# Peak products of the 64-wide cross attention as pairs of 64-row operands into both banks, with one maximum over two banks

## What is computed

```
heads, dim_head = (16, 64)
x = layer_norm(x, ln_m_g, ln_m_b)              # context, 2 x 4096 x 256
lat = layer_norm(latents, ln_l_g, ln_l_b)      # 2 x 256 x 256
q = lat @ Wq
kv_input = jnp.concatenate([x, lat], axis=1)   # 4352 keys
k, v = jnp.split(kv_input @ Wkv, 2, axis=-1)
dots = jnp.einsum('bhid,bhjd->bhij', q, k) * dim_head ** (-0.5)
attn = jax.nn.softmax(dots, axis=-1)
out = jnp.einsum('bhij,bhjd->bhid', attn, v)
```

## Time and profile before

| what | value |
|---|---|
| median of 3 runs | 4079.12 us (4075.48 to 4081.56) |
| the profiled execution's own time | 4080.47 us |
| span of its instructions | 4078.7 us |
| TensorE (PE) busy | 3406.9 us, 84% |
| VectorE (DVE) busy | 2315.1 us, 57% |
| ScalarE (ACT) busy | 1529.1 us, 37% |
| GpSimd (POOL) busy | 810.1 us, 20% |
| peak products L1259 | 191.0 us busy, 576 weight loads |
| their maxima L1428 | 374.8 us busy, x576 |
| mean granted TensorE clock | 0.908 of full |

### The profile page before, as it was taken

One profiled execution on the slowest core, in us unless ns is written; L12 is line 12 of the kernel. 1 busy time (PEld: TensorE's weight loads), 2 busy tenths in 40 slices (PEclk: granted clock), 3 DMA queues, 4 the chain that ended last, 5 costly groups with the idle time before them and its releaser, 6 DMA issues. The chain is left out here.

```text
span 4078.7 us, 55851 instructions
## 1 busy us (share of the span) xinstructions
PE 3406.9 (84%) x21132; PEld 2130.0 (52%) x21188; DVE 2315.1 (57%) x3897; ACT 1529.1 (37%) x2241; POOL 810.1 (20%) x572
## 2 busy tenths in 40 slices
PE   7878895999999699999759587899857579995759
PEld 5546684656656466566525375444446434442225
DVE  1144413655655656656368413899654279984963
ACT  2223311334334243343246321467633137773311
POOL 0000000254255152453218202000000110000420
PEclk9888897999999799999879788999977789997879
DMA  2245463000000100000187513765200285540001
GB/s 94 85 142 181 166 238 140 16 6 6 6 1 1 55 6 9 4 4 1 30 272 260 218 68 105 164 122 106 50 21 26 103 205 114 120 81 21 0 22 59
DMA packets 223953, 339.07 MB, mean 83 GB/s; under 512 B 104272, under 2 KB 177680, under 8 KB 218064
## 3 DMA queue, kind: packets, MB, share of 16 engines
q1 hardware_dynamic: 223312, 334.56, 28.1%
q0 software_dynamic: 384, 1.05, 0.1%
HBM read 257.95 MB, written 77.63 MB: 82 GB/s over the span
## 5 line engine op out<-in xcount | busy, mean ns | idle before, releaser
L1428 DVE TENSOR_REDUCE L1x_pk<-L1x_psm 128x1 f32<-128x512 f32 (+1 forms) x576 | 374.8, 661 | 177.1 <-PE L1x_psm L1259 170.0
L1229 POOL TENSOR_TENSOR L1x_acc<-L1x_acc,L1x_pr 128x512 f32<-128x512 f32 x256 | 416.4, 1627 | 137.3 <-ACT L1x_pr L1404 118.9
L1404 ACT ACTIVATE L1x_pr<-L1x_pss 128x1024 f32<-128x1024 f32 x272 | 278.6, 1024 | 285.4 <-PE L1x_pss L1316 277.8
L1450 DVE TENSOR_TENSOR L1x_acc<-L1x_acc,L1x_pr 128x512 f32<-128x512 f32 x256 | 261.1, 1020 | 202.0 <-ACT L1x_pr L1404 197.6
L955 DVE TENSOR_REDUCE L2x_pk<-L2x_psm 128x1 f32<-128x512 f32 x512 | 328.1, 685 | 38.1 <-PE L2x_psm L792 34.3
L955 DVE TENSOR_REDUCE L3x_pk<-L3x_psm 128x1 f32<-128x512 f32 x512 | 328.1, 685 | 32.5 <-PE L3x_psm L792 28.7
L932 ACT ACTIVATE L2x_pr<-L2x_pss 128x1024 f32<-128x1024 f32 x256 | 248.2, 1021 | 105.6 <-PE L2x_pss L833 105.3
L932 ACT ACTIVATE L3x_pr<-L3x_pss 128x1024 f32<-128x1024 f32 x256 | 248.1, 1021 | 100.6 <-PE L3x_pss L833 100.3
L1316 PE MATMUL L1x_pss<-L1x_Q,L1x_K 64*128 64x256 f32 x2176 | 279.3, 376 | 0.0
L1282 PE MATMUL L1x_pss<-L1x_w,L1x_cT 128*128 128x256 f32 x1088 | 278.4, 380 | 0.8
L1277 PE MATMUL L1x_pss<-L1x_cT,L1x_w 128*128 128x512 f32 (+1 forms) x576 | 277.4, 572 | 0.8
(11 more groups left out here) (653 smaller groups left out, 5991.2 us busy)
## 6 DMA issues: line engine op xcount, KB each, us to landing
f0e_wt<-in_f_pieces SPq DMA_DIRECT2D x10, 3072.0 KB, 11.4
offset_rows<-s_rows SPq DMA_DIRECT2D x32, 768.0 KB, 3.4
L2x_KS<-L2x_key_parts SPq DMA_DIRECT2D x24, 1024.0 KB, 13.1
L3x_KS<-L3x_key_parts SPq DMA_DIRECT2D x24, 1024.0 KB, 13.1
s_add<-offset_rows SPq DMA_DIRECT2D x32, 512.0 KB, 3.8
n_cT<-in_ctxT SPq DMA_DIRECT2D x32, 512.0 KB, 5.3
f1e_wt<-in_f_pieces SPq DMA_DIRECT2D x8, 2048.0 KB, 15.0
L2x_key_parts<-n_kst SPq DMA_DIRECT2D x32, 384.0 KB, 3.1
```

The source lines that it names most:

```text
L1229: i = nc.gpsimd.tensor_tensor(acc[:, n, 1, :, :], acc[:, n, 1, :, :], pr[:, A % RING, :, 1, :], ALU.add)
L1404: nc.scalar.activation(pr[:, A % RING, :, :, :].rearrange("p h e q -> p (h e q)"), pss[:, x:x + 2, :].rearrange("p h n -> p (h n)"), ACT.E ...
L1428: nc.vector.reduce_max(pk[:, m, hq, j:j + 1], psm[:, i % 2, 0:NQ[j][1]], AX).then_inc(peak_read, 1)
L1450: i = nc.vector.tensor_tensor(acc[:, n, 0, :, :], acc[:, n, 0, :, :], pr[:, A % RING, :, 0, :], ALU.add)
```

## The change

The zero-filled copies go. `Qb` holds the bf16 queries as they are, both heads over 128 partitions. A peak product becomes a pair: head 0 with partitions 0 to 63 into bank 0 of `psm`, head 1 with partitions 64 to 127 into bank 1, with one signal after the second. VectorE takes one maximum over both banks, 128 x 2 x 512 in and 128 x 2 out. There are 36 pairs per group instead of 72 products. Since a pair takes both banks, it waits for the maximum of the pair before (and not of the last but one), and the first pair of a group waits for `o_done`, which before only the second product did. `peaks_by` hands out half as many per tile. The memset of `qzb` and a third of the query copies go.

```
-    PART = NB * 4
+    PART = NB * QT
     PEAKS = KC * PART
-    QEV = 3 * KC
+    QEV = 2 * KC
...
-        qzb = t.sb(pre + "_qzb", [P, 2, KC, 2, S], BF16)
+        Qb = t.sb(pre + "_Qb", [P, 2, KC, S], BF16)
...
-            @block.vector
-            def _(dve):
-                nc.vector.memset(qzb[:, :, :, :, :], 0.0)
...
-                pk = u.sb(pre + "_pk", [P, KC, 4, NB])
+                pk = u.sb(pre + "_pk", [P, KC, QT, 2, NB])
...
-                    return min(PEAKS, 4 * (t_ - 1), -(-PEAKS * (t_ - 1) // (TILES - 2)))
+                    return min(PEAKS, 2 * (t_ - 1), -(-PEAKS * (t_ - 1) // (TILES - 2)))
...
                             if i == 0:
                                 pe.wait_ge(q_ev, QEV * (g + 1))
-                            if hq == 0:
+                                if g >= 1:
+                                    pe.wait_ge(o_done, KC * g)
+                            if qt == 0:
                                 pe.wait_ge(k_cast, NK * g + m * NB + j + 1)
-                            if i == 1 and g >= 1:
-                                pe.wait_ge(o_done, KC * g)
-                            if i >= 2:
-                                pe.wait_ge(peak_read, PEAKS * g + i - 1)
-                            nc.tensor.matmul(psm[:, i % 2, 0:w_], qzb[:, g % 2, m, h, qt * P:(qt + 1) * P], Kb[:, m, o:o + w_],
-                                             start=True, stop=True).then_inc(peaks, 1)
+                            if i >= 1:
+                                pe.wait_ge(peak_read, PEAKS * g + i)
+                            for h in range(2):
+                                half = slice(64 * h, 64 * h + 64)
+                                p = nc.tensor.matmul(psm[:, h, 0:w_], Qb[half, g % 2, m, qt * P:(qt + 1) * P], Kb[half, m, o:o + w_],
+                                                     start=True, stop=True)
+                            p.then_inc(peaks, 1)
...
-                            for h in range(2):
-                                half = slice(64 * h, 64 * h + 64)
-                                nc.vector.tensor_copy(qzb[half, g % 2, m, h, :], psm[half, 0, m * S:(m + 1) * S]).then_inc(q_ev, 1)
+                            nc.vector.tensor_copy(Qb[:, g % 2, m, :], psm[:, 0, m * S:(m + 1) * S]).then_inc(q_ev, 1)
...
-                            nc.vector.reduce_max(pk[:, m, hq, j:j + 1], psm[:, i % 2, 0:NQ[j][1]], AX).then_inc(peak_read, 1)
+                            nc.vector.reduce_max(pk[:, m, qt, :, j], psm[:, :, 0:NQ[j][1]], AX).then_inc(peak_read, 1)
                             if i % PART == PART - 1:
                                 dve.wait_ge(peak_read, PEAKS * g + i + 1)
-                                link(nc.vector.reduce_max(mx[:, m, :], pk[:, m, :, :], AX))
+                                link(nc.vector.reduce_max(mx[:, m, :], pk[:, m, :, :, :].rearrange("p t h j -> p (t h) j"), AX))
```

More of the change, by code:

```diff
@@ L1189, in peaks_by @@
                         return 0
-                    return min(PEAKS, 4 * (t_ - 1), -(-PEAKS * (t_ - 1) // (TILES - 2)))
+                    return min(PEAKS, 2 * (t_ - 1), -(-PEAKS * (t_ - 1) // (TILES - 2)))
                 def peak_of(i):
                     m, rest = divmod(i, PART)
-                    j, hq = divmod(rest, 4)
-                    return m, j, hq
+                    j, qt = divmod(rest, QT)
+                    return m, j, qt
                 @block.sync
@@ L1247, in peak_products @@
                         for i in range(first, last):
-                            m, j, hq = peak_of(i)
-                            h, qt = divmod(hq, 2)
+                            m, j, qt = peak_of(i)
                             o, w_ = NQ[j]
@@ L1294, in peak_rows @@
                             for qt in range(QT):
-                                i = nc.tensor.matmul(pst[64 * h:64 * h + 1, qt * P:(qt + 1) * P], mx[:, m, 2 * h + qt:2 * h + qt + 1],
+                                i = nc.tensor.matmul(pst[64 * h:64 * h + 1, qt * P:(qt + 1) * P], mx[:, m, 2 * qt + h:2 * qt + h + 1],
                                                      k.ident[:, :], start=True, stop=True)
```

## The result

The changed kernel takes 4118.56 us (median of 4 runs, 4114.55 to 4119.68), the kernel before 4078.56 on the same chip (4075.48 to 4081.56). The ratio is 1.0094, with a 95% interval of 1.0078 to 1.0111: 40.0 us or 0.9% slower. The forecast was 4121, in a range of 4102 to 4134. The profiled execution took 4114.55 us; its span is 4112.7, against 4078.7.

The account below looks back on a forecast made before the run. Taking TensorE's stream to bound the tile stretch, the prediction summed -58.7 (columns), +83.8 (switches) and +16.6 (stalls) to +41.7 us on 4080.5, giving 4122, less 1.4 for the median: 4121 us, range 4102 to 4134.

Parts of the forecast that it names:

- Fewer columns: In the tiles, 64-row pairs run side by side, each costing one stream of 0.216 us; 58.7 us saved in all.
- Rival B: In the tiles, pair halves run in turn without overlap, so 58.7 us isn't saved: about 4170 us; chance 2%.
- Two switches per pair: In the tiles, each 64-row pair costs TensorE 0.305 us for changing the array's shape and back; 83.8 us added.
- Tile 21 and the last pair: The last pair's switches lie in TensorE's wait for ACT's copy; after tile 21, 0.20 us is already paid before.
- Rival A: In the tiles, shape changes cost nothing because weights load beneath the other kind's product: faster, 4052 us; chance 4%.
- rival D: Whole kernel: no change that can be told, within 0.2% or 8 us, overhead 0.09 to 0.16 per pair; chance 3%.
- the exchange: In the tiles, swapping two 128-row products for one 64-row pair loses by itself: 0.52 us against 0.43.
- One buffer: Pairs wait for the previous maximum (1.22 us): six 0.32 us tile stalls per group at half-tile distances, 15.4 us added.
- Rival C: VectorE sets the pace in the tiles, its two-bank maximum taking over 1.76 us; at 2.0 us, 4212 us; chance 3%.
- The averages: In tile 2 of groups 1 to 3, the first pair waits 1.44 us for the normalization, 8.6 us added.
- the old waits that are gone: Stalls of the kernel before, at the averages (5.0 us) and at the narrow tile (2.4 us), disappear.
- The rest at nothing: Fewer query copies, the dropped memset and VectorE's shorter busy time lie in slack and change the kernel's time by nothing.

Follow-up runs that it names:

- x2: x1 with both query tiles' pairs issued together, 18 visits to the 64-row shape per group in place of 36: 4054.55 us, 0.9923 of the kernel before.
- x1: Changed kernel with a second two-bank buffer, so a pair waits for the last maximum but one: 4094.76 us, 1.0023 of the kernel before.
- x4: x1 with the old zero-padded 128-row operands, two products in place of each pair: 4074.05 us, 0.9973 of the kernel before.
- x3: Changed kernel with the old zero-padded 128-row operands, still one buffer and one maximum over both banks: 4115.05 us, 1.0068 of the kernel before.
- y1: Changed kernel with two maxima of one bank each in place of one over both: 4125.41 us, 1.0107 of the kernel before.
- y2: Changed kernel with the same pairs scheduled otherwise, none in the middle of tile 2: 4118.38 us, 1.0091 of the kernel before.

## Why the prediction was right

**Fewer columns: right.** The halves of a pair start within 7 ns of each other, and the pair holds one stream of 0.216. Rival B needed starts 0.2 apart and falls.

**Two switches per pair: right.** The pair holds 0.10 over its stream, the first fp32 record behind it another 0.10, the last fp32 record to the next pair 0.10: 0.30, where 0.305 was taken from the earlier trace rows. The forecast's worry, that a single short pair would behave otherwise than two together, came to nothing: as x2 shows, the cost belongs to the visit. Tile 21 and the last pair are as forecast. Rival A needed 0.22 from pair to fp32 product, and rival D an overhead of 0.09 to 0.16. x1 against x4 shows that the exchange alone loses. The Trainium skill, "TensorEngine Tiling (Array Packing)", Key Properties, says that a change of the tiling mode drains TensorE; the idle loads of 0.23 and 0.76 and the square above agree, though they don't tell a drain from a weight load that merely isn't issued ahead. Its Theoretical Speedup, up to twofold for contractions of 64 rows or fewer, is there in the stream of a pair, and is lost again where one pair stands alone between 128-row products. x2's second pair, 0.23 behind the first, is what comes near it.

**One buffer: right, slightly low.** The maximum takes 1.226 where 1.22 was taken, the short distances are the six per group that the schedule function gave, and no other pair waits. Four of the six stalls are 0.33 and two 0.42. The two are pairs that start a new block of keys (tiles 13 and 24) and so carry a second wait, on `k_cast`, which has long been met. TensorE in tile 13 of the second group, changed kernel:

```profile
910.71 1.13 PE L1275 MATMUL L1x_pss<-L1x_cT,L1x_w 128*128 128x512 f32 x2
912.20 0.39 PE L1256 MATMUL L1x_psm<-L1x_Kb,L1x_Qb 64*128 64x512 bf16 x2 [0.36 <-DVE L1x_pk L1424]
912.52 1.13 PE L1275 MATMUL L1x_pss<-L1x_cT,L1x_w 128*128 128x512 f32 x2
913.91 0.39 PE L1256 MATMUL L1x_psm<-L1x_Kb,L1x_Qb 64*128 64x512 bf16 x2 [0.27 <-DVE L1x_pk L1424]
```

The pair at 912.20 carries both waits, the one at 913.91 only that for the maximum. Rival C needed a maximum over 1.76.

**The averages: right.** 1.48 instead of 1.44; here too the pair waits on more than one semaphore and starts 0.11, not 0.06, behind the end of line 1454.

**The sum.** Forecast per group 3.15 + 1.92 + 1.44 - 0.84 - 0.30 = 5.37, measured 5.57. For the first group 4.77, measured 4.95. In all 41.8 against 43.3. Term by term in groups 1 to 3: the exchange 3.20 against 3.15; the six stalls 2.17 (four of 0.33, two of 0.42) against 1.92, the largest miss, most of it at the two pairs with two waits; the averages 1.48 against 1.44; the old waits that are gone 1.03 + 0.25 = 1.28 (x4 against before, and what x4 itself still waits) against 1.14. The medians differ by 40.0; that this lies within 2 us of the forecast is in part the scatter of the rest of the program.

The rest at nothing: right. The two query copies that go show nowhere, as the 78.35 and 78.36 above say; without the memset the first tile phase starts at 729.39 and not 729.57, which is within the scatter. (The forecast's "two fewer per unit" should read per group; its 16 copies in all are right.)

What isn't shown: why a wait on two semaphores, of which one is met, is 0.05 to 0.09 longer. It was seen in all eight groups, in x3, y1 and y2 too, and not isolated by a kernel of its own.

## What to carry to other kernels

Price a change of TensorE's shape by the visit, from the start of the last product of one shape to the second of the other, and compare it with the stream that it saves: here 0.30 us a visit against 0.22 a pair, so that one pair per visit loses and two gain. When an edit merges two buffers into one, count the places where less work lies between two uses than the reader takes, and what else used the second buffer; here 6 of 36 distances and one `o_done` cost more than the whole exchange of shapes. A shifted schedule can put the short distances elsewhere, as in y2, so list them all again.

## What the runs showed of the hardware

- A visit to the 64-row shape between fp32 128-row products costs 0.10 on the way in, 0.10 on the way out and 0.10 more between the first two fp32 records, where the loads say that the first fp32 weights are loaded in the open (741.32, with the product). Between two bf16 pairs of the same shape (x2) the next weights are loaded beneath, the second pair starts 0.23 behind the first, and the visit costs no more for it than its stream of 0.216.
- VectorE's maximum over two banks in one instruction, 1024 columns, takes 1.226 us; two of 512 in a row take 1.29, since the second starts 0.08 before the first ends.
- A product that waits for VectorE with two waits started 0.09 us later than one with a single wait (0.42 against 0.33); that the second wait is the reason is not isolated.
